# A new order of stages on four engines, and new homes for shared PSUM banks, in a pipelined RWKV and FP4 FFN kernel

## The reference

```
h = layernorm(x) * (1 + ca) + sa
x = x + ga * rwkv(h)          # two layers, each a time mix and a channel mix, then a layer norm
h = layernorm(x) * (1 + cb) + sb
x = x + gb * fp4_ffn(h)       # gate, up and down projections on FP4 quantized values, width 704
```

```
out_t   = r_t (state + u k_t v_t)
state   = state * w_t + k_t v_t
```

## Time and profile before

| | |
|---|---|
| median of 3 runs | 3035.34 us (3033.44 to 3035.51) |
| profiled execution | 3035.34 us |
| its span on the core | 3033.6 us |
| TensorE busy | 2770.6 us, 91% |
| VectorE busy | 2351.6 us, 78% |
| ScalarE busy | 1379.8 us, 45% |
| GpSimd busy | 1287.4 us, 42% |
| mean granted TensorE clock | 0.968 |

### The profile page before, as it was taken

How to read it: one execution, slowest core, us unless ns; L and a number is a source line. 1 busy time by engine, 2 the same in 40 slices (tenths; PEclk the granted TensorE clock), 3 DMA queues, 4 the chain that set the end, 5 groups by cost and what they waited for, 6 DMA issues and landing times.

```text
span 3033.6 us, 78728 instructions
## 1 busy us (share of the span) xinstructions
PE 2770.6 (91%) x32829; PEld 2209.1 (73%) x32829; DVE 2351.6 (78%) x5345; ACT 1379.8 (45%) x2707; POOL 1287.4 (42%) x1457
## 2 busy tenths in 40 slices
PE   5568999999999999999999999999999999999865
PEld 3456777777777777777777777777777777777653
DVE  4555888888888888888888888888888888888654
ACT  1234554454445545545454454455544544455321
POOL 3234444444444444444444544444445444444310
PEclk8679999999999999999999999999999999999977
DMA  4000000000000000000000000000000000000000
GB/s 147 14 5 5 9 9 12 12 12 12 12 5 9 12 12 12 12 12 9 9 9 12 12 12 12 12 9 9 9 12 12 12 12 12 5 12 9 8 8 7
DMA packets 36311, 41.51 MB, mean 14 GB/s; under 512 B 2748, under 2 KB 34680, under 8 KB 35960
## 3 DMA queue, kind: packets, MB, share of 16 engines
q1 hardware_dynamic: 35696, 36.32, 3.8%
q10 hardware_dynamic: 264, 0.16, 0.0%
HBM read 28.08 MB, written 8.39 MB: 12 GB/s over the span
## 4 chain that ended last, share of the span: by engine, by line
PE 77%; DVE 9%; ACT 8%; issue 5%; POOL 1%; DMA 0%; ACTq 0%; DVEq 0%; POOLq 0%
PE ps_all L1300 12%; PE ps_all L1113 11%; PE ps_all L1121 10%; PE ps_all L1333 9%; PE ps_all L1314 6%; PE ps_all L1220 5%; PE ps_all L1351 5%; PE ps_all L1105 3%; PE ps_all L1152 2%; PE ps_all L1137 2%; ACT mixin L754 2%; PE ps_all L1215 2%; PE ps_all L1246 2%; PE ps_all L1276 2%; PE ps_all L1141 1%
## 5 line engine op out<-in xcount | busy, mean ns | idle before, releaser
L593 POOL TENSOR_TENSOR mixin<-mixin,hT_tm 128x512 f32<-128x512 f32 x320 | 388.4, 1223 | 353.5 <-DVE mixin L946 353.5
L1300 PE MATMUL ps_all<-chan,cwk 128*128 128x256 f32 x1536 | 378.9, 394 | 13.1 <-DVE chan L925 11.2
L981 DVE TENSOR_TENSOR sxrk<-sxrk,dec 128x512 f32<-128x512 f32 x384 | 270.7, 705 | 111.9 <-PE ps_all L1220 110.0
L1314 PE MATMUL ps_all<-cwv,chan 128*128 128x256 f32 x1536 | 344.0, 381 | 0.0
L1300 PEld LDWEIGHTS ps_all<-chan,cwk 128*128 128x128 f32 x1536 | 286.1, 193 | 70.0 <-issue 28.0
L1314 PEld LDWEIGHTS ps_all<-cwv,chan 128*128 128x128 f32 x1536 | 290.8, 191 | 38.8 <-issue 0.2
L575 POOL TENSOR_TENSOR rstd<-var,powc 128x2 f32<-128x2 f32 x224 | 186.9, 834 | 251.2 <-DVE var L887 250.8
L946 DVE SCALAR_TENSOR_TENSOR mixin<-ps_all,vcol,sxrk 128x256 f32<-128x256 f32 x640 | 269.6, 475 | 27.0 <-PE ps_all L1152 13.6
L1220 PEld LDWEIGHTS ps_all<-sxrk 64*64 64x64 f32 x10240 | 170.2, 131 | 137.3 <-issue 137.1
L612 POOL TENSOR_TENSOR lora<-S,dec 128x256 f32<-128x256 f32 x128 | 93.0, 726 | 373.1 <-DVE S L996 373.0
L1220 PE MATMUL ps_all<-sxrk 64*64 64x32 f32 x10240 | 202.9, 218 | 45.1 <-DVE att L987 45.1
(11 more groups left out here) (181 smaller groups left out, 6269.4 us busy)
## 6 DMA issues: line engine op xcount, KB each, us to landing
xin<-in_L_attn_x_dram SPq DMA_DIRECT2D x32, 256.0 KB, 2.7
tok<-in_L_attn_x_dram SPq DMA_DIRECT2D x32, 256.0 KB, 2.7
out_dram<-x SPq DMA_DIRECT2D x32, 256.0 KB, 2.1
cwk<-in_L_attn_cWk_dram SPq DMA_DIRECT2D x2, 768.0 KB, 7.9
cwv<-in_L_attn_cWv_dram SPq DMA_DIRECT2D x2, 768.0 KB, 10.0
ffn_work<-in_L_wmod_dram SPq DMA_DIRECT2D x2, 512.0 KB, 6.2
tok<-in_L_ffn_w_down_dram SPq DMA_DIRECT2D x1, 704.0 KB, 4.1
tok<-in_L_ffn_w_gate_dram SPq DMA_DIRECT2D x1, 640.0 KB, 8.0
```

Of the source, the lines that this page charges most:

```text
L593: pool.tensor_tensor(m, m, hT["tm", l][:, :, :, 1:P + 1].rearrange("p k c t -> p (k c) t"), ALU.add).then_inc(ev["mixed"][b], 1)
L981: v.tensor_tensor(rko, rko, t, ALU.mult).then_inc(ev["rk_lev"][b], 1)
L1300: ins = pe.matmul(bank(b, "ck", lj, "k")[:, m * TT:(m + 1) * TT], cwk[:, l, k, n:n + P], k_in[:, k, :], start=(k == 0), stop=(k == KC - 1))
L1314: ins = pe.matmul(bank(b, "cv", l, "v")[:, c * D:(c + 1) * D], relu[t // 2][:, t % 2, c * P:(c + 1) * P], cwv[:, l, t, :], start=(t == 0), ...
```

## The change

Nothing of the stages themselves is changed. The four lists of `ORDER` are written anew: each starts at another point of the cycle, and in each some stages stand elsewhere among their neighbours. In ScalarE's list the longest lag is 5 turns (6 before). In `SECOND` other stages use bank 7: `mf.2` of stream 0, `ck.1` of stream 3 and one half of `ht.0` go to bank 6 and so on, and `so`, `cv`, `xt` and the other half of `ht.0` come to bank 7.

```diff
--- before.py
+++ after.py
@@ -24,25 +24,24 @@
 
 PE, DVE, AC, POOL = "PE", "DVE", "ACT", "POOL"
 ORDER = {
-    PE: """4/4 gu.1.1; 1/2 lev.1; 0/1 yt; 3/3 cr cv; 0/1 wo; 1/2 pv lev.2; 4/4 ht.1; 1/2 lev.3; 2/1 turn.cm; 4/4 dn; 1/2
-        pg; 2/1 ck.0; 0/0 turn.tm; 1/2 lev.4; 2/1 ck.1 ck.2; 0/0 mix; 1/2 lev.5; 0/0 mf.0 mf.1 mf.3 mf.2; 1/2 lev.6; 2/1
-        cr; 1/2 kt; 0/0 pw1; 1/2 so ov; 0/0 pk pr pw2; 1/2 yt; 2/1 cv; 1/2 wo; 4/3 xt; 0/0 lev.1; 4/3 gu.0.0; 0/0 pv
-        lev.2; 1/1 turn.tm; 4/3 gu.0.1; 0/0 lev.3; 3/2 turn.cm; 0/0 pg; 1/1 mix mf.0 mf.1 mf.3 mf.2; 3/2 ck.0; 0/0
-        lev.4; 1/1 pw1; 3/2 ck.1; 1/1 pk; 0/0 lev.5; 1/1 pr; 4/3 ht.0; 0/0 lev.6; 1/1 pw2; 0/0 kt; 4/3 gu.1.0; 0/0 so
-        ov; 3/2 ck.2""",
-    DVE: """0/1 h0; 1/3 lev.3; 0/1 lna.tm; 2/2 cmix; 0/1 lnb.tm; 4/5 dn; 4/4 lna.out; 1/3 pg lev.4; 0/1 mix; 4/4 lnb.out x2;
-        1/3 lev.5; 0/1 mf.0; 1/3 lev.6; 0/1 mf.1; 4/4 lna.ffn; 1/3 st.0; 0/1 mf.3 mf.2; 1/3 st.1 gna; 4/4 lnb.ffn; 1/3
-        gnb; 4/4 hf qa.x qc.x; 2/2 cv; 0/1 mf.4; 1/3 wo; 1/2 lna.tm; 0/1 lev.1; 3/3 lna.cm; 1/2 lnb.tm; 4/4 gu.0.0; 3/3
-        lnb.cm; 0/1 lev.2; 4/4 gu.0.1; 1/2 mix; 0/1 lev.3; 4/4 qa.0; 3/3 cmix; 1/2 mf.0 mf.1 mf.3; 0/1 pg lev.4; 1/2
-        mf.2; 4/4 qc.0; 0/1 lev.5 lev.6; 4/4 gu.1.0; 0/1 st.0 st.1; 1/2 mf.4; 0/1 gna gnb; 4/4 gu.1.1 qa.1; 1/2 lev.1;
-        4/4 qc.1; 3/3 cv; 0/1 wo; 2/1 lna.cm; 1/2 lev.2; 2/1 lnb.cm; 0/0 lna.in lnb.in""",
-    AC: """0/3 kt; 1/4 pw2; 0/3 gna; 3/5 ck.2; 4/6 gu.1.1; 0/3 yt; 4/6 qa.1; 3/5 cr; 4/6 ht.1; 2/3 turn.cm; 1/4 pv pg; 0/2
-        turn.tm; 2/3 ck.0 ck.1 ck.2; 0/2 mix; 2/3 cr; 1/4 kt; 0/2 pw1; 1/4 gna; 0/2 pk pr; 1/4 yt; 4/5 qa.x; 0/2 pw2;
-        4/5 xt gu.0.0; 1/3 turn.tm; 0/2 pv; 4/5 gu.0.1; 3/4 turn.cm; 1/3 mix; 0/2 pg; 4/5 qa.0; 3/4 ck.0; 1/3 pw1; 3/4
-        ck.1; 1/3 pk; 4/5 ht.0; 1/3 pr; 4/5 gu.1.0""",
-    POOL: """4/5 lna.out; 0/2 mf.0; 1/4 st.0; 0/2 mf.1; 1/4 st.1; 0/2 mf.3; 4/5 lna.ffn; 1/4 gnb; 0/2 mf.2; 1/4 yt; 2/3 cv;
-        0/2 mf.4; 1/3 lna.tm; 0/2 tot; 3/4 lna.cm; 1/3 mix; 3/4 cmix; 1/3 mf.0 mf.1; 0/2 st.0; 1/3 mf.3; 0/2 st.1 gnb;
-        1/3 mf.2 mf.4 tot; 0/2 yt; 3/4 cv; 2/2 lna.cm; 0/1 lna.in; 2/2 cmix; 0/1 lna.tm; 4/5 dn; 0/1 mix""",
+    PE: """1/2 pk; 0/1 lev.5; 3/3 ck.1 ck.2 cr; 0/1 lev.6; 4/4 ht.0; 0/1 kt; 1/2 pr; 0/1 so ov; 4/4 gu.1.0 gu.1.1; 1/2 pw2;
+        0/1 yt; 3/3 cv; 1/2 lev.1 pv; 4/4 ht.1; 0/1 wo; 1/2 lev.2; 4/4 dn; 2/1 turn.cm; 1/2 lev.3 pg lev.4; 2/1 ck.0;
+        0/0 turn.tm; 2/1 ck.1; 1/2 lev.5; 2/1 ck.2; 1/2 lev.6; 2/1 cr; 1/2 kt; 0/0 mix; 1/2 so ov; 0/0 mf.0 mf.1 mf.3
+        mf.2; 2/1 cv; 0/0 pw1; 1/2 yt; 0/0 pk pr pw2; 4/3 xt; 1/2 wo; 4/3 gu.0.0; 0/0 lev.1 pv; 1/1 turn.tm; 4/3 gu.0.1;
+        3/2 turn.cm; 0/0 lev.2; 1/1 mix; 0/0 lev.3; 1/1 mf.0 mf.1 mf.3 mf.2; 0/0 pg; 3/2 ck.0; 1/1 pw1; 0/0 lev.4""",
+    DVE: """1/3 lev.2; 2/2 lnb.cm; 0/1 lna.in lnb.in h0; 1/3 lev.3; 0/1 lna.tm; 2/2 cmix; 0/1 lnb.tm; 4/5 dn; 1/3 pg lev.4;
+        4/4 lna.out; 1/3 lev.5; 4/4 lnb.out; 1/3 lev.6; 0/1 mix; 4/4 x2 lna.ffn; 1/3 st.0; 4/4 lnb.ffn; 1/3 st.1; 4/4
+        hf; 0/1 mf.0 mf.1; 1/3 gna; 4/4 qa.x; 1/3 gnb; 0/1 mf.3; 2/2 cv; 4/4 qc.x; 0/1 mf.2; 1/3 wo; 1/2 lna.tm; 0/1
+        mf.4; 3/3 lna.cm; 1/2 lnb.tm; 4/4 gu.0.0; 3/3 lnb.cm; 0/1 lev.1; 4/4 gu.0.1; 1/2 mix; 0/1 lev.2; 3/3 cmix; 1/2
+        mf.0; 0/1 lev.3; 1/2 mf.1 mf.3; 0/1 pg; 1/2 mf.2; 0/1 lev.4; 4/4 qa.0; 0/1 lev.5; 4/4 qc.0; 0/1 lev.6 st.0 st.1
+        gna; 4/4 gu.1.0; 0/1 gnb; 4/4 gu.1.1 qa.1; 1/2 mf.4; 4/4 qc.1; 3/3 cv; 1/2 lev.1; 0/1 wo; 2/1 lna.cm""",
+    AC: """0/2 pk pr; 4/5 xt; 0/2 pw2; 4/5 gu.0.0; 1/3 turn.tm; 4/5 gu.0.1; 3/4 turn.cm; 0/2 pv; 1/3 mix; 0/2 pg; 3/4 ck.0;
+        4/5 qa.0; 3/4 ck.1 ck.2; 1/3 pw1; 3/4 cr; 4/5 ht.0; 1/3 pk; 0/2 kt; 1/3 pr; 0/2 gna; 4/5 gu.1.0 gu.1.1; 1/3 pw2;
+        4/5 qa.1; 0/2 yt; 4/5 ht.1; 1/3 pv; 2/2 turn.cm; 1/3 pg; 2/2 ck.0; 0/1 turn.tm; 2/2 ck.1 ck.2; 1/3 kt; 2/2 cr;
+        0/1 mix; 1/3 gna; 0/1 pw1; 4/4 qa.x; 1/3 yt""",
+    POOL: """3/4 lna.cm; 0/2 tot st.0; 1/3 mix; 3/4 cmix; 1/3 mf.0 mf.1 mf.3; 0/2 st.1 gnb; 1/3 mf.2; 0/2 yt; 1/3 mf.4; 3/4
+        cv; 1/3 tot; 2/2 lna.cm; 1/3 st.0; 0/1 lna.in; 2/2 cmix; 0/1 lna.tm; 4/5 dn; 0/1 mix; 4/4 lna.out lna.ffn; 1/3
+        st.1; 0/1 mf.0; 1/3 gnb; 0/1 mf.1 mf.3; 1/3 yt; 2/2 cv; 0/1 mf.2; 1/2 lna.tm; 0/1 mf.4""",
 }
 
 def schedule(L, NC, LEVELS, KH):
@@ -103,8 +102,8 @@
 SHARED_PSUM = [("mf.2", "m"), ("so", "t"), ("turn.cm", "x"), ("ck.0", "k"), ("ck.1", "k"), ("ck.2", "k"), ("cr", "r"), ("cv", "v"), ("xt", "x"), ("dn", "o")]
 SHARED_PSUM += [(f"gu.{c}.{u}", use) for c in range(2) for u in range(2) for use in "gu"] + [(f"ht.{c}", use) for c in range(2) for use in "ab"]
 
-SECOND = """0 mf.2 m; 2 turn.cm x; 2 ck.0 k; 2 ck.2 k; 3 turn.cm x; 3 ck.0 k; 3 ck.1 k; 3 ck.2 k; 3 cv v; 4 gu.0.0 g; 4 gu.0.1 g; 4 ht.0
-    b; 4 gu.1.0 u; 4 gu.1.1 u; 4 ht.1 b"""
+SECOND = """0 so t; 2 turn.cm x; 2 ck.0 k; 2 ck.2 k; 2 cv v; 1 so t; 3 turn.cm x; 3 ck.0 k; 3 ck.2 k; 3 cv v; 4 xt x; 4 gu.0.0 g; 4
+    gu.0.1 g; 4 ht.0 a; 4 gu.1.0 u; 4 gu.1.1 u; 4 ht.1 b"""
 SECOND = {" ".join(x.split()) for x in SECOND.split(";")}
 
 
```

## The result

The changed kernel took 3057.0 us (median of 4, 3056.5 to 3061.5) against 3034.4 us (3033.3 to 3035.5): a ratio of 1.0069, with a 95% interval of 1.0051 to 1.0087. It is slower by 22.6 us. The forecast was slower by 44 us. The direction and the mechanism came as forecast, the size did not: the ratio of the forecast was 1.0147. With the later sessions the changed kernel ran 13 times, 3046.7 to 3062.5 us, median 3056.5: it spreads more than the kernel before, so a difference of a few us to it shows nothing by itself.

The account below looks back on a forecast made before the run. TensorE was taken to carry the 87.1 us period, waiting only 2.4 us of it. Removing these waits and adding 1.3 + 1.8 + 0.9 us made +1.6 us, 28 times: 3035 + 44 = 3079 us, range 3044 to 3115.

Parts of the forecast that it names:

- What the change removes: TensorE's short waits at `mf`, `lev.3`, `so` and `lev.1` of layer 0: 2.4 us saved per period, remainders booked separately.
- the forecast remainder of `mf`: At `mf` of layer 1, with only a 0.60 us `lev.3` as cover: about 0.15 us of wait stays.
- Stretch 1: From the end of `wo` to `ck.0` of layer 0, VectorE's list outlasts TensorE's cover: 1.3 us new wait, between 1.2 and 1.9.
- Stretch 2: From the end of `wo` to `mix` of layer 1, VectorE's list outlasts TensorE's: 1.8 us new wait, between 1.5 and 2.2.
- Small new returns: Short new waits at `kt`, `gu.1.1`, `mf` of layer 1, `yt`, `ht.0`: together 0.9 us, between 0.2 and 1.5.
- Sum of the period: Per period −2.4 + 1.3 + 1.8 + 0.9 = +1.6 us, 88.7 us instead of 87.1; 28 times, +44 us.
- Fill and tail I leave unchanged: Before the first and behind the 28th down projection: no change, a tile taking 323 us against 324; ±10 us allowed.
- the sign that I had named for it: Wrong if the steady period is as forecast and the first down projection differs from 387 us by more than 10 us.
- rival (d): TensorE's clock falls below the full grant in the stretches with waits; given nothing of its own, no chance stated.

Follow-up runs that it names:

- moving `pv`: Changed kernel with `pv` of layer 1 on TensorE behind `wo` of layer 0 instead of ahead of `ht.1`: 3055.9 us, ratio 1.0073.
- the reordering: Changed kernel with `pv` of layer 0 on TensorE ahead of `gu.0.0` instead of behind `lev.1`: 3069.3 us, ratio 1.0118.
- the added piece: Changed kernel with two unused statistics instructions on VectorE ahead of `lna.tm` of layer 1, between `wo` and `mix`: 3075.8 us, ratio 1.0139.
- its control: Changed kernel with the same two unused statistics instructions on VectorE ahead of `wo` of layer 1, where it stands idle: 3057.1 us, ratio 1.0068.
- the run with stretch 1 in the old order: Changed kernel with TensorE's stages from `wo` to `ck.0` of layer 0 in the old order, `lev.4` still ahead of `ck.0`: 3101.0 us, ratio 1.0219.
- the old banks: Changed kernel's lists of `ORDER` with the bank homes (`SECOND`) of the kernel before: 3114.5 us, ratio 1.0262.

## Why the prediction was right in kind and wrong in size

The forecast was +44 us, measured are +22.6. Some 13 us of the difference lie in the terms of the period, stretch 2 and the small returns above all, and some 8 us in the step that left the fill unchanged.

**What the change removes.** Right. Of the three returns of `mf`, `lev.3` and `so` the forecast remainder of `mf` is left, 2.1 us over 13.6 periods, 0.15. The fourth, at `lev.1`, is in the sum of stretch 2.

**Stretch 1.** Right in place and nearly in size: 1.17 us against 1.3, where the working itself gave 10.3 less 9.2, 1.1. Its two sides were both 0.4 us short. From the end of `wo` to `ck.0` VectorE's side took 1687.18 to 1697.89, 10.7 us (10.3 forecast), mostly since the scaling of 0.70 us (1510.72 in the kernel before) took 1.03. GpSimd's state product on line 611 had started 0.06 us before it (1690.57 us, 0.61 us long); in the kernel before no instruction of GpSimd ran beside it, and I had not followed that one. TensorE's took 9.6 us (9.2 forecast). That the errors cancelled was luck. That this is the only chain there was an error of the working that did not show in the sum; moving `pv` showed it.

**Stretch 2.** Right in mechanism: the reordering, the added piece and its control all say that VectorE's list sets the sum. Mis-sized: 1.47 us where I took 1.8. VectorE's side with its hand-overs came as forecast, 10.8 us against 10.9, but TensorE's cover was 9.4 us (10.84 less 1.42) and not 9.2. GpSimd, for which I had added 0.1 us, does not show in the view of waits.

**Small new returns.** Mis-sized: `kt` 0.17, `mf` 0.15, `pw2` 0.19 (not forecast), `lev` 0.15, together 0.66 us where I took 0.9. `gu.1.1`, `yt` and `ht.0` do not wait in the steady part.

**Sum of the period.** 3.3 us of new waits, not 4.0: 0.7 us less than forecast, half of it in stretch 2. That alone would make +0.9. Measured is +1.15, by two things that the sum left out. TensorE's own work was not the same: its busy time per period is 84.1 us before and 84.6 after, +0.5, for which no run gives the reason. And the idle time that is left went only from 3.0 to 3.65 us, since idle pieces too short for the view of waits, some 0.6 us per period before, nearly all went or grew into it (the 4.1 us at line 1275 were there before, as pieces of 0.14 us). Against the forecast of +1.6 us per period this is 13 us over 28 periods.

**"Fill and tail I leave unchanged".** This step failed. The period makes +31 us and the whole only +22.6, so the fill gave back some 8 us; the profiled execution, 3 us under its median, has 12. This was within the ±10 us that I allowed, and the sign that I had named for it (a steady period as forecast, and a first down projection more than 10 us from 387) is what came. I had compared the latency of a tile along TensorE's list, 323 against 324 us, as if the list were full. In the fill it is not. With one tile in flight the question is which stage of the second tile stands ahead of a stage of the first: in the old list `cv` waits behind `pk`, `pr` and `pw2` of the second tile, whose inputs are late. Moving that one stage made the one kernel 6 us faster and the other 9 us slower.

**The clock, rival (d).** In the steady part of the profiled executions of both kernels the grant stays full, so it played no part in what they show. That I gave it nothing was wrong as a rule: it shows in four experiments, and once each in two more.

## What to carry to other kernels

In software-pipelined lists, where engines work on different tiles each in its own fixed order, find each point where one engine must stand until the other has come to it (an anchor). From one such point on add up both lists to the next, and compare; a wait moved within such a stretch is not a wait removed. Look for all anchors before adding cover, since the second longest chain may be only tenths of a us behind. Do the fill separately, with the list of the one or two tiles that are really there.

## What the runs showed of the hardware

The granted clock of TensorE fell in the steady part of four experiments, mostly behind two waits close together. In the run with stretch 1 in the old order, windows around the `dn` of 6.76 us (granted clock, DMA share and GB/s stand last):

```profile
1537.00:1539.50 2.50, 1.37 (x36) 1.32 (x37) 1.94 (x6) 0.73 (x2) 1.18 (x2) 0.89 0.00 0
1539.50:1542.00 2.50, 2.50 (x8) 2.03 (x7) 2.27 (x6) 2.18 (x4) 1.90 (x2) 0.50 0.03 7
1542.00:1544.00 2.00, 2.00 (x10) 1.70 (x9) 2.00 (x6) 0.15 (x1) 0.00 (x0) 0.90 0.00 0
```

Before it TensorE had waited 0.80 and 0.78 us with 32 small matmuls on a quarter of the array between them. Then it was busy all the time at half the grant, 1.2 instead of 2.4 GHz, for some 3 us, and `dn` took 1.4 us more. It happened in 5 of the 25 periods from 500 to 2750 us. Summed over 3 us windows of that part the missing grant is 8.6 us there, 20.5 us in the run with `pv` of layer 0 first (a wait of up to 1.5 us at `turn.cm`) and 18.8 us with `mf.4` first; it is 5.1 us with the old banks, and none in the kernel before and in the changed one. The 20.5 us fit the reordered stretch 2, which was slower at the same sum of waits: 12 us by the medians, and 24 us in this profiled execution (3077.5 against 3053.6). Its four executions have a mean grant of 0.962 to 0.964, those of the changed kernel 0.968 to 0.971. That the fall is the cause is argued: no run has that order with a full grant. With `mf.4` first and with stretch 1 in the old order, too, part of the loss is the clock. In the two runs with `cv` of the first tile late and with the piece ahead of the stretch, whose steady order on TensorE is that of the changed kernel, the grant fell once each, behind a single wait of 1.4 and 1.7 us inside `so ov` for which the profile names no cause. So the changed kernel's order is not safe from it either. That waits of 0.8 us, two close together, or a single one of 1.4 us can be followed by a fall of the clock I had not expected; in most periods the same waits were not.

A full-width stage of TensorE is 0.1 us longer behind a stage on quarters of the array: `dn` takes 5.29 us to the next start behind `lev.2` (1687.78 to 1693.07) and 5.19 behind `turn.cm`. All of it lies in the first matmul, 0.32 us to the next start instead of 0.22. The new list has such neighbours in stretch 1, which is part of the longer cover there. It does not explain the 0.5 us of work per period: counted over 2000 us of both traces, both lists have 12 such neighbours per period.
